# Eight products that nobody reads, put on TensorE at the end of each attention batch

## The chip, the cores and the metric

The kernel runs on one core of one Trainium2 chip. The metric is the device time of that core in microseconds (us), the median over the runs of a kernel. PE is TensorE, DVE is VectorE, ACT is ScalarE, POOL is GpSimd, SP is SyncE.

## The reference

A hybrid block on an array of 16 x 16 x 16 x 64: a gated scan convolution, an attention of 16 heads, and a graph attention that weighs four experts. Only the attention touches the change:

```python
x = x + _L0_conv_ref(_gn(x), ...)
t = _to_tokens(x)                       # 16 batches of 256 tokens, 64 channels
t = t + _L1_attn_ref(_ln_t(t), ...)     # 16 heads of 4 channels
t = t + _L1_ffn_ref(_ln_t(t), ..., edge_index)
...
qkv = (x @ w_qkv + b_qkv).reshape(b, n, 3, H, D)
attn = softmax(einsum('bhqd,bhkd->bhqk', q, k))
out = einsum('bhqk,bhkd->bhqd', attn, v)
```

## The kernel before

Every engine has its own program, written out by hand, and they meet only through semaphores. The attention runs over 16 batches in a software pipeline: in its turn i an engine works on the scores of batch i and on the exponentials and values of batch i - 1. The flags of a turn are `one` (there is a batch i, turns 0 to 15), `two` (there is a batch i - 1, turns 1 to 16) and `three` (there is a batch i + 1).

A turn on PE has eight rounds. A round makes transposed scores of the last batch, two heads each (`scores_t`, L646, into PSUM banks 2 to 5), scores of this batch for two heads (`scores`, L631, banks 0 and 1), in every other round the operands of the next batch (`expand`, L598, bank 7), and the products with the values (`pv`, L615, f32, bank 6). DVE takes the row maxima of each head's scores (L1259) and, beside them, does a piece of a sort that the graph stage needs (`aside`, L1158 and L1159 in the middle batches); POOL prepares that piece. ACT takes the exponentials (L915).

Behind the eighth round the maxima are complete. DVE negates them and splits them into three bf16 parts, a chain of small instructions on which each waits for the last (L1264 to L1285). PE waits for the end of that chain and turns the parts (L669, eight 128-column products):

```python
                if one:

                    pe.wait_ge(mz_ready, i + 1)
                    for g in range(G):
```

DVE adds them to the queries (L1289, `q2`), and `scores_t` of the next turn needs `q2`. PE goes on with the transposes of the last batch's output (L679), then with the first two rounds of the next turn, which have little work since no exponentials are there yet. Behind the attention come the rest of the sort, the experts' products (L730 to L748), and the graph stage. The turns 4 to 12 stand in a hardware loop; between turn 12 and turn 13 all engines do a step of the sort (L687).

Of the kernel before, what the change touches and what calls it, by code (L numbers as in the profile page):

```python
# [23 lines left out]
CH = 512  # L24
# [60 lines left out]
def build(nc, a, cf, cb, jpat, out):  # L85
    ctx = ExitStack()
    with ctx:
# [7 lines left out]
        ps = psum[:]  # L95
# [20 lines left out]
        def select(side, g2):  # L116

            return cB[0:96, (2 * side + g2) * P:(2 * side + g2 + 1) * P]
# [33 lines left out]
        stack = work[0:96, 3:7, :].bitcast(BF16)  # L152
# [184 lines left out]
        def later(i, first):  # L337

            return not isinstance(i, int) or i > first
# [196 lines left out]
        def _(pe):  # L536
# [11 lines left out]
            for w in range(3):  # L548
                if w == 2:
                    pe.wait_ge(s_act, NCH)  # L550
                for c in range(NCH):
                    pe.matmul(ps[:, 4 * (w % 2) + c, :], wbd[:, w, :], xn[:, c * CH:(c + 1) * CH],
                              start=True, stop=True).then_inc(s_z, 1)
# [17 lines left out]
            for c in range(NCH):  # L571
                pe.wait_ge(ln_out, c + 1)
                for u in range(U):
                    pe.matmul(ps[:, u * 4 + c, :], wqkv[C * u:C * u + C, 0:2 * C], tn[C * u:C * u + C, cs(c)],
                              start=True, stop=True).then_inc(s_qk, 1)
            pe.wait_ge(s_qkf, 8)
            for b in range(B):
                for u in range(U):
                    n = b * U + u
# [6 lines left out]
            def expand(i, buf, s):  # L586


                if s > 0:
                    pe.wait_ge(qke_ready, i * 4 + s)  # L590
                elif later(i, 2):
                    pe.wait_ge(o_done, i - 2)
                elif i in (1, 2):
                    pe.wait_ge(qke_ready, 4 * i)
                if s == 0 and isinstance(i, int) and i < 2:
                    pe.wait_ge(stacked[i], STACKED[i])
                for g2 in range(2):
                    mm = pe.matmul(ps[:, 7, g2 * 256:(g2 + 1) * 256], select(s // 2, g2), stack[:, s, bass.ds(i * 256, 256)],  # L598
                                   start=True, stop=True)
                mm.then_inc(ex_ready, 1)  # L600

            def pv(i, buf, m):

                pe.wait_ge(exp_done, i * 8 + m + 1)
                if m == 0:
                    pe.wait_ge(staged, i + 1)
                    if later(i, 0):
                        pe.wait_ge(o_done, i)
                if m == 4:
                    pe.wait_ge(oe_done, i * 2 + 1)  # L610
                g = m // 2
                for kt in range(U):
                    for jj in range(2):
                        j = 2 * (m % 2) + jj
                        mm = pe.matmul(ps[32 * j:32 * j + 32, 6, (g % 2) * 256:(g % 2 + 1) * 256],  # L615
                                       vstage[:, buf, kt, 4 * g + j, :], pbuf[:, m % 4, jj, kt, :],
                                       start=(kt == 0), stop=(kt == 1))
                mm.then_inc(pv_done, 1)

            def scores(i, buf, h):  # L620

                if h == 0:
                    pe.wait_ge(qke_ready, i * 4 + 4)
                if h < 2 and later(i, 0):
                    pe.wait_ge(q2_ready, i * 2 - 1 + h)
                if h >= 2 or later(i, 0):
                    pe.wait_ge(mx_done, i * 16 + h - 1)
                g, j = h // 4, h % 4
                r = slice(32 * j, 32 * j + 32)
                for qt in range(U):  # L630
                    mm = pe.matmul(ps[:, h % 2, qt * 256:(qt + 1) * 256],  # L631
                                   qke[r, buf, 0, g, qt * P:(qt + 1) * P], qke[r, buf, 1, g, :],
                                   start=True, stop=True)
                mm.then_inc(s1_ready, 1)

            def scores_t(i, buf, m):

                if m % 4 == 0:
                    pe.wait_ge(q2_ready, i * 2 + 1 + m // 4)
                if m >= 2 or later(i, 0):  # L640
                    pe.wait_ge(exp_done, i * 8 + m - 1)
                for kt in range(U):
                    for jj in range(2):
                        g, j = m // 2, 2 * (m % 2) + jj
                        r = slice(32 * j, 32 * j + 32)
                        mm = pe.matmul(ps[:, 2 + 2 * (m % 2) + jj, kt * 256:(kt + 1) * 256],  # L646
                                       qke[r, buf, 1, g, kt * P:(kt + 1) * P], q2[r, g, :],
                                       start=True, stop=True)
                mm.then_inc(s2_ready, 1)

            def body(i, buf, one, two, three):
                for m in range(8):
                    if two:
                        scores_t(i - 1, (buf + 2) % 3, m)
                    if one:
                        scores(i, buf, 2 * m)
                        scores(i, buf, 2 * m + 1)
                    if three and m % 2:
                        expand(i + 1, (buf + 1) % 3, m // 2)
                    if two and m >= 1:  # L660
                        pv(i - 1, (buf + 2) % 3, m - 1)
                if two:
                    pv(i - 1, (buf + 2) % 3, 7)
                if one:

                    pe.wait_ge(mz_ready, i + 1)
                    for g in range(G):
                        for qt in range(U):
                            mm = pe.matmul(ps[:, g // 2, (g % 2) * 256 + qt * P:(g % 2) * 256 + (qt + 1) * P],  # L669
                                           mz[:, qt, g, :, :].rearrange("p j r -> p (j r)"), identb, start=True, stop=True)  # L670
                    mm.then_inc(mt_ready, 1)
                if two:

                    pe.wait_ge(oe_done, (i - 1) * 2 + 2)
                    if three:
                        pe.wait_ge(qke_ready, i * 4 + 8)
                    for qt in range(U):
                        for g in range(G):
                            mm = pe.transpose(ps[:, 6 + qt, g * P:(g + 1) * P], ots[:, g, qt * P:(qt + 1) * P], ident)  # L679
                    mm.then_inc(ot_ready, 1)  # L680
# [11 lines left out]
            for g in range(G):  # L692
                expand(0, 0, g)
            pe.wait_ge(s_v1, 2)
            batches(pe, body, turn_slots)
            pe.wait_ge(o_done, B)
            for b in range(B):
# [122 lines left out]
            with pe.If(overflow(pe) > 0):  # L820
                pe.wait_ge(gen_start, 1)
                for u in range(U):
                    for c in range(NCH):
                        mm = pe.matmul(ps[0:NF, 4 * u + c, :], wext[C * u:C * u + C, :], tn[C * u:C * u + C, c * CH:(c + 1) * CH],
                                       start=True, stop=True)
# [15 lines left out]
            for u in range(U):  # L841
                for k in range(8):
                    for q in range(4):
                        r = slice(32 * q, 32 * q + 32)
                        mm = pe.matmul(ps[:, 4 + q, u * 16:(u + 1) * 16], move[r, u, 112 - 16 * k:240 - 16 * k], gv[r, k],
                                       start=(k == 0), stop=(k == 7))
# [797 lines left out]
```

## Time and profile before

| | |
|---|---|
| median of 3 runs | 1025.7 us (1022.24 to 1026.14) |
| the profiled execution | 1031.22 us, its span 1029.5 us |
| PE busy | 644.5 us, 63% of the span |
| DVE busy | 762.1 us, 74% |
| ACT / POOL busy | 306.7 us / 499.9 us |
| mean granted clock of PE | 0.748 |

The page gives busy times of the engines, the clock that PE was granted (1.0 is 2.4 GHz, 0.5 is 1.2 GHz), and the chain of work that ended last. A matmul's time in the profile is that of one product from its start to its end, and products overlap; so a group of eight has a start and a length of its own. "Idle before" names the idle time of the engine just before a group and what ended it.

### The profile page before, as it was taken

The page shows a single profiled execution, that of the slowest core. Times are in us where ns is not written, and L with a number is a line of the kernel's source. Part 1 is how long each engine was busy: PE and PEld are TensorE (multiplying, and loading weights), DVE is VectorE, ACT ScalarE, POOL GpSimd, SP SyncE. Part 2 cuts the span into 40 slices and gives each one's busy share as a digit, 9 for nine tenths or more (in the row PEclk, how much of TensorE's full clock was granted, in tenths as well). Part 3 has the DMA queues.
Part 4 walks back from the last instruction along what each step waited for, and adds up shares of the span by engine and source line. Part 5 has one row for each costly group of instructions (what it writes and reads, how often), then busy time and mean ns, then how long its engine had stood idle before and what let it go on. Part 6 is the DMA issues. An engine that isn't in the chain of part 4 may idle for free.

```text
span 1029.5 us, 15298 instructions
## 1 busy us (share of the span) xinstructions
PE 644.5 (63%) x5984; PEld 331.3 (32%) x5984; DVE 762.1 (74%) x1477; ACT 306.7 (30%) x463; POOL 499.9 (49%) x399
## 2 busy tenths in 40 slices
PE   1501472499788888997787969999999410003421
PEld 1200130133333333333333445555656210002421
DVE  3999887697886877667888779998989831008775
ACT  1510350144554645444444431111111010000015
POOL 3990000017676766650000028888888877756000
PEclk9955875556987977669767969999999855555655
DMA  5010004100000000000000222000000000110001
GB/s 152 0 43 6 8 9 99 24 1 1 1 2 1 1 1 0 0 0 0 2 1 1 82 48 53 6 6 7 6 6 7 7 10 10 10 7 1 3 2 41
DMA packets 22001, 17.08 MB, mean 17 GB/s; under 512 B 13488, under 2 KB 18944, under 8 KB 21168
## 3 DMA queue, kind: packets, MB, share of 16 engines
q1 hardware_dynamic: 15424, 14.02, 5.1%
q0 software_dynamic: 5392, 2.18, 2.6%
q8 instruction: 42, 0.69, 0.3%
q10 hardware_dynamic: 1120, 0.00, 0.1%
q14 instruction: 23, 0.19, 0.1%
HBM read 10.51 MB, written 2.54 MB: 13 GB/s over the span
## 4 chain that ended last, share of the span: by engine, by line
PE 41%; DVE 30%; issue 13%; ACT 4%; SPq 2%; another core or an unknown queue 0%; DMA 0%; DVEq 0%; POOL 0%; ACTq 0%; POOLq 0%
PE psum L615 11%; PE psum L748 10%; DVE mx L1259 7%; PE psum L631 4%; DVE arena L1323 3%; PE psum L646 3%; PE psum L739 3%; PE psum L730 3%; SPq L381 2%; DVE arena L1289 2%; PE psum L598 2%; DVE arena L1030 2%; ACT arena L1004 1%; DVE arena L1026 1%; PE psum L669 1%
## 5 line engine op out<-in xcount | busy, mean ns | idle before, releaser
L493 POOL DMA_INDIRECT work<-node_rows,idx x160 | 257.8, 1611 | 53.1 <-issue 48.5
L1259 DVE TENSOR_REDUCE mx<-psum 128x2 f32<-128x512 f32 x256 | 164.3, 683 | 69.8 <-PE psum L631 67.9
L1323 DVE TENSOR_TENSOR arena<-arena 128x4096 bf16<-128x4096 bf16 (+1 forms) x128 | 182.0, 1486 | 18.1 <-PE psum L748 13.9
L915 ACT ACTIVATE arena<-psum 128x1024 f32<-128x1024 f32 x128 | 129.4, 1024 | 158.4 <-PE psum L646 158.4
L615 PE MATMUL psum<-arena 128*32 128x256 f32 x1024 | 168.3, 486 | 2.3 <-DVE arena L1299 1.4
L470 POOL TENSOR_SCALAR work<-arena,cF 128x184 f32<-128x184 f32 x128 | 93.7, 744 | 129.0 <-DVE arena L1159 73.2
L748 PE MATMUL psum<-arena 128*32 128x128 bf16 x2048 | 131.3, 420 | 4.3 <-DVE arena L1323 3.2
L631 PE MATMUL psum<-arena 32*128 32x256 bf16 x512 | 85.5, 340 | 27.5 <-DVE mx L1259 24.5
L748 PEld LDWEIGHTS psum<-arena 128*32 128x32 bf16 x2048 | 78.2, 149 | 43.6 <-DVE arena L1323 11.6
L615 PEld LDWEIGHTS psum<-arena 128*32 128x32 f32 x1024 | 56.8, 130 | 75.6 <-issue 57.8
L461 POOL COPY arena<-arena 128x160 f32<-128x160 f32 x16 | 5.4, 348 | 136.9 <-DVE arena L1145 91.7
L472 POOL TENSOR_TENSOR work<-work,arena 128x368 f32<-128x368 f32 x64 | 61.8, 965 | 5.3
L790 PE MATMUL psum<-arena,work 128*128 128x32 bf16 x192 | 10.0, 188 | 84.5 <-issue 84.5
L646 PE MATMUL psum<-arena 32*128 32x256 bf16 x512 | 59.9, 331 | 3.0 <-DVE work L1173 1.3
L949 ACT ACTIVATE arena<-psum,b1c 128x512 f32<-128x512 f32 x32 | 21.6, 686 | 133.5 <-PE psum L730 133.5
L1415 DVE COPY work<-psum 92x2048 f32<-92x2048 f32 x1 | 2.3, 2287 | 73.9 <-PE psum L790 73.9
L631 PEld LDWEIGHTS psum<-arena 32*128 32x128 bf16 x512 | 33.4, 113 | 61.6 <-DVE mx L1259 47.1
L412 POOL PARTITION_ALL_REDUCE over<-over x1 | 0.4, 377 | 94.4 <-DVE over L1228 94.4
L598 PE MATMUL psum<-work,arena 96*128 (+1 forms) x128 | 31.3, 336 | 23.8 <-DMA work<-work 21.7
L739 PEld LDWEIGHTS psum<-w,arena 128*128 128x128 f32 x256 | 31.8, 195 | 27.1 <-issue 19.9
L739 PE MATMUL psum<-w,arena 128*128 128x64 f32 x256 | 36.2, 286 | 3.1 <-ACT arena L949 3.1
L560 PE MATMUL psum<-work,cF 128*128 128x512 f32 x8 | 5.2, 804 | 50.5 <-DVE work L1090 50.5
(290 smaller groups left out, 989.7 us busy)
## 6 DMA issues: line engine op xcount, KB each, us to landing
work<-work SPq DMA_DIRECT2D x48, 64.0 KB, 2.0
work<-node_rows,idx POOLq DMA_INDIRECT x160
arena<-in_L_ffn_edge_index_dram SPq DMA_DIRECT2D x2, 1024.0 KB, 10.6
work<-edge_nodes SPq DMA_DIRECT2D x4, 368.0 KB
digits<-arena SPq DMA_DIRECT2D x1, 1024.0 KB, 4.0
arena<-digits SPq DMA_DIRECT2D x1, 1024.0 KB, 4.9
arena<-in_jpat_dram SPq DMA_DIRECT2D x1, 1024.0 KB, 6.8
out_dram<-work SPq DMA_DIRECT2D x4, 256.0 KB, 2.3
```

The lines of the kernel that those rows point to most:

```text
L470: gp.step(pool.tensor_scalar(upto[:, pair % 4, n, :], own, upper[:, 2 * pair + n:2 * pair + n + 1], None, ALU.is_le))
L472: pool.tensor_tensor(upto[:, pair % 4, :, :], upto[:, pair % 4, :, :], own.rearrange("p (n l) -> p n l", n=1).broadcast_to([P, 2, CAP]), A ...
L493: pool.indirect_dma_start(gath[:, l, :], None, tab, bass.IndirectOffsetOnAxis(ap=idx[:, l:l + 1], axis=0)).then_inc(done, 16)
L598: mm = pe.matmul(ps[:, 7, g2 * 256:(g2 + 1) * 256], select(s // 2, g2), stack[:, s, bass.ds(i * 256, 256)], start=True, stop=True)
L615: mm = pe.matmul(ps[32 * j:32 * j + 32, 6, (g % 2) * 256:(g % 2 + 1) * 256], vstage[:, buf, kt, 4 * g + j, :], pbuf[:, m % 4, jj, kt, :], ...
L631: mm = pe.matmul(ps[:, h % 2, qt * 256:(qt + 1) * 256], qke[r, buf, 0, g, qt * P:(qt + 1) * P], qke[r, buf, 1, g, :], start=True, stop=True)
L646: mm = pe.matmul(ps[:, 2 + 2 * (m % 2) + jj, kt * 256:(kt + 1) * 256], qke[r, buf, 1, g, kt * P:(kt + 1) * P], q2[r, g, :], start=True, st ...
L739: mm = pe.matmul(ps[:, 2 + m % 2, t * C:(t + 1) * C], hid[:, m % 4, t * P:(t + 1) * P], w2[:, e, :], start=True, stop=True)
L748: mm = pe.matmul(ps[r, 7, 0:HB], oh[:, buf, HB:HB + LB, c], oh[:, buf, 0:HB, c], start=first and c < 4, stop=last and c >= HC - 4)
L915: act.activation(pbuf[:, m % 4, :, :, :], ps[:, 2 + 2 * (m % 2):4 + 2 * (m % 2), :].rearrange("p j (k q) -> p j k q", k=U), ACT.Exp).then_ ...
L1259: v.reduce_max(mx[:, h, :], ps[:, h % 2, :].rearrange("p (u k) -> p u k", u=U), AX.X).then_inc(mx_done, 1)
L1323: ins = v.tensor_tensor(oh[:, buf, first:first + n, :], hl2[:, s_, bass.ds(blk * HC, HC)].rearrange("p (j c) -> p j c", j=1).broadcast_to( ...
```

## The change

In turns 1 to 15 PE does eight more products between the last `pv` and the wait for `mz_ready`. Each has a stationary operand of 96 x 128 (`select(0, 0)`, bf16) and 512 bf16 columns of `stack`, and writes a PSUM bank from 2 to 5, which holds transposed scores that ACT has read by then. None waits for a semaphore and none raises one. Nothing reads the results: the next `scores_t` writes over them.

```diff
--- before.py
+++ after.py
@@ -661,6 +661,9 @@
                         pv(i - 1, (buf + 2) % 3, m - 1)
                 if two:
                     pv(i - 1, (buf + 2) % 3, 7)
+                if one and two:
+                    for n in range(8):
+                        pe.matmul(ps[:, 2 + n % 4, :], select(0, 0), stack[:, 0, 0:CH], start=True, stop=True)
                 if one:
 
                     pe.wait_ge(mz_ready, i + 1)
```

PE's program around turn 0, `-` before and `+` after; the waits are in brackets, and names behind `<-` are memory (`work` holds `stack`, `arena` the selecting matrices):

```order
 L598 MATMUL psum<-work,arena 128x256 [waits qke_ready]
 L598 MATMUL psum<-work,arena 128x256
-L669 MATMUL psum<-arena,mz 128x128 [waits mz_ready]
-L669 MATMUL psum<-arena,mz 128x128 x7
+L672 MATMUL psum<-arena,mz 128x128 [waits mz_ready]
+L672 MATMUL psum<-arena,mz 128x128 x7
 L646 MATMUL psum<-arena 128x256 [waits q2_ready]
 L646 MATMUL psum<-arena 128x256 x3
```

Turn 0 gets nothing; the lines only have other numbers (L669 is L672 now). The same engine at the end of turn 1:

```order
 L615 MATMUL psum<-arena 32x256 [waits exp_done]
 L615 MATMUL psum<-arena 32x256 x3
-L669 MATMUL psum<-arena,mz 128x128 [waits mz_ready]
-L669 MATMUL psum<-arena,mz 128x128 x7
-L679 MATMUL psum<-cF,arena 128x128 [waits qke_ready,oe_done]
-L679 MATMUL psum<-cF,arena 128x128 x7
+L666 MATMUL psum<-work,arena 128x512 x8
+L672 MATMUL psum<-arena,mz 128x128 [waits mz_ready]
+L672 MATMUL psum<-arena,mz 128x128 x7
+L682 MATMUL psum<-cF,arena 128x128 [waits qke_ready,oe_done]
+L682 MATMUL psum<-cF,arena 128x128 x7
```

The new L666 stands behind the last L615, whose wait for `exp_done` it is queued after, and ahead of the wait for `mz_ready`. This piece is repeated in every turn up to 15. The last turn, 16, gets nothing. The programs of DVE, ACT, POOL and SP are the same but for line numbers.

## Rows read from the trace of the kernel before

**Rows 1.** Page part 2: granted clock of PE in tenths, 40 slices.
```profile
PEclk9955875556987977669767969999999855555655
```

**Rows 2.** Waits of PE: total us, times, longest.
```profile
PE psum L669 <- DVE mr L1285: 30.2, 16, 3.0
```

**Rows 3.** Windows: length, busy us per engine, granted clock, DMA share, GB/s.
```profile
234.00:484.11 250.11, 218.63 (x1673) 91.71 (x1673) 187.90 (x484) 125.97 (x154) 151.54 (x196) 0.77 0.00 1
484.11:577.00 92.89, 74.33 (x566) 32.19 (x568) 79.27 (x254) 40.82 (x47) 0.93 (x2) 0.78 0.00 1
```

**Rows 4.** Windows from one start of L669 to the next.
```profile
345.00:365.06 20.06, 17.10 (x152) 7.54 (x153) 16.91 (x44) 11.38 (x14) 14.75 (x20) 0.91 0.00 0
...
438.04:464.60 26.56, 23.35 (x152) 9.24 (x153) 17.56 (x44) 11.54 (x15) 15.13 (x20) 0.66 0.00 0
464.60:484.11 19.51, 17.12 (x153) 7.62 (x153) 15.58 (x40) 11.38 (x14) 0.35 (x1) 0.91 0.00 0
484.11:512.00 27.89, 20.01 (x164) 8.76 (x165) 24.68 (x80) 11.60 (x14) 0.93 (x2) 0.85 0.00 1
512.00:536.00 24.00, 21.57 (x151) 8.89 (x148) 20.45 (x71) 11.52 (x14) 0.00 (x0) 0.67 0.01 1
536.00:561.50 25.50, 19.29 (x152) 8.91 (x153) 20.69 (x65) 9.17 (x11) 0.00 (x0) 0.80 0.01 1
561.50:577.00 15.50, 13.46 (x106) 5.63 (x105) 13.45 (x39) 8.54 (x9) 0.00 (x0) 0.78 0.01 1
```

**Rows 5.** Windows: the parts of the batch from 345.00 to 365.06.
```profile
345.00:346.60 1.60, 1.54 (x18) 1.31 (x20) 0.89 (x2) 0.00 (x0) 0.62 (x1) 1.00 0.00 0
346.60:350.20 3.60, 2.40 (x24) 0.92 (x26) 3.53 (x11) 2.34 (x3) 0.59 (x1) 1.00 0.00 0
350.20:353.60 3.40, 3.40 (x22) 1.06 (x18) 2.48 (x7) 1.21 (x2) 3.27 (x5) 0.51 0.00 0
353.60:363.36 9.76, 9.76 (x96) 4.24 (x94) 8.50 (x20) 7.24 (x9) 8.64 (x12) 1.00 0.00 0
363.36:365.06 1.70, 0.00 (x1) 0.00 (x1) 1.51 (x9) 0.59 (x1) 1.62 (x3) 1.00 0.00 0
```

**Rows 6.** Timeline, end of that batch: start, us, engine, line, idle before.
```profile
361.90 1.46 PE L615 MATMUL psum<-arena 128*32 128x256 f32 x16
...
364.85 0.15 DVE L1285 COPY mr<-mr 128x1 f32<-128x1 f32 x1
...
365.06 0.62 PE L669 MATMUL psum<-arena,mz 128*128 128x128 bf16 x8 [1.70 <-DVE mr L1285]
```

**Rows 7.** Timeline of DVE: three pairs of maxima in that batch.
```profile
349.42 1.27 DVE L1259 TENSOR_REDUCE mx<-psum 128x2 f32<-128x512 f32 x2
...
352.12 1.29 DVE L1259 TENSOR_REDUCE mx<-psum 128x2 f32<-128x512 f32 x2 [0.92 <-PE psum L631]
...
354.44 1.29 DVE L1259 TENSOR_REDUCE mx<-psum 128x2 f32<-128x512 f32 x2 [0.51 <-PE psum L631]
```

**Rows 8.** Timeline: L669 of two batches that end at half clock.
```profile
233.97 1.03 PE L669 MATMUL psum<-arena,mz 128*128 128x128 bf16 x8 [1.50 <-DVE mr L1285]
...
438.04 1.03 PE L669 MATMUL psum<-arena,mz 128*128 128x128 bf16 x8 [0.61 <-DVE mr L1285]
```

**Rows 9.** Windows around two other falls of the clock.
```profile
389.89:391.20 1.31, 1.31 (x16) 1.26 (x16) 0.58 (x1) 0.00 (x0) 0.00 (x0) 1.00 0.00 0
391.20:404.80 13.60, 12.82 (x74) 4.29 (x74) 8.61 (x22) 6.12 (x7) 7.54 (x10) 0.50 0.00 0
...
438.04:442.40 4.36, 3.23 (x30) 2.14 (x30) 3.15 (x9) 1.91 (x3) 0.00 (x0) 0.89 0.01 2
442.40:459.40 17.00, 16.89 (x92) 5.81 (x94) 9.52 (x22) 7.39 (x10) 11.89 (x16) 0.50 0.00 0
```

**Rows 10.** The chain of work: L703, eight passes of 512 f32 columns.
```profile
582.21 3.44 PE psum L703 x8
```

**Rows 11.** Page part 5: the maxima on DVE, busy us, mean ns, idle before.
```profile
L1259 DVE TENSOR_REDUCE mx<-psum 128x2 f32<-128x512 f32 x256 | 164.3, 683 | 69.8 <-PE psum L631 67.9
```

## The prediction

> **What bounds the kernel now.** I read the page first, then the waits of PE, then windows cut at the starts of L669, then the timeline of one batch. The page's clock line shows the attention (slices 9 to 22, 26 us each) at 5 to 9 tenths: PE changes between its two levels, 2.4 GHz (1.0) and 1.2 GHz (0.5), all the time [rows 1]. The windows say how much: over the eleven batches from 234.00 to 484.11 the granted clock is 0.77, over the rest of the attention 0.78 [rows 3]. A mean of 0.77 means that (1 - 0.77) x 2 = 46% of 250.11 us, 115 us, ran at half clock.
>
> What half clock costs is seen by comparing batches. The one from 345.00 to 365.06 takes 20.06 us at 0.91; the one from 438.04 to 464.60 takes 26.56 us at 0.66. DVE works 16.91 and 17.56 us in them, nearly the same [rows 4]. So the difference is PE: at half clock a round is bound by PE, and DVE waits for scores; at full clock DVE is nearly the bound.
>
> The batch from 345.00 shows where the clock is lost [rows 5]. L669 and L679 fill PE up to 346.60. Then it is thinly used (2.40 of 3.60 us), because the first rounds wait for DVE's `q2` and maxima and have no values to multiply. At 350.20 the clock falls, for 3.40 us. Then 9.76 us of unbroken work at full clock, and at the end PE sits idle for 1.70 us, waiting for the negated maxima; this wait occurs 16 times, 30.2 us in all, 3.0 us at most [rows 2]. So in each batch there are two thin places, the idle one ahead of L669 and the one behind L679, with only 1.6 us of dense work between. What PE did before a fall: in this batch the second thin place, after the first. At 391.20 the clock fell only 1.3 us behind L669, right behind the idle place [rows 9]. The batch from 345.00 also had such a wait ahead of it (16 waits in 16 turns [rows 2]), and yet stayed at 1.00 until 350.20 [rows 5]: there the idle place alone did not drop the clock. I conclude that both thin places count together, and the change fills the first one.
>
> **The new products' own cost.** Each has 512 columns, eight have 4096. L669 has 8 x 128 = 1024 columns and takes 0.62 us at full clock [rows 6], 1.03 at half [rows 8]; the 0.41 between is what 1024 columns gain by twice the clock, so they cost 0.43 at 2.4 GHz and 0.85 at 1.2. Four times that: 1.71 us at full clock, 3.41 at half. An upper bound at full clock: the eight f32 passes of 512 columns at L703 take 3.44 us [rows 10]. I take 1.71, since these are bf16 as L669 is. Their weight loads lie beside the products as L669's do.
>
> At full clock the last value product ends at 363.36, and L669 starts at 365.06, 0.06 after the 0.15 us of L1285 from 364.85 have ended [rows 6]. The idle time is 1.70, the new work 1.71. It just fits; queued behind it are L669 and, through `q2`, all of the next batch. I take 0.1 us of delay a batch, bounds 0 and 0.3: 14 x 0.1 = 1.4 us. At half clock 3.41 us meet idle times of 1.50 and 0.61 [rows 8]: 1.9 to 2.8 us late. Turn 1 arrives at half clock (L669 takes 1.03 at 233.97). The dense work may raise the clock on its way, as it did inside the L669 and L679 of 438.04 (0.89 over 4.36 us [rows 9]); I take 1.0, bounds 0 and 1.9.
>
> **What a batch costs when the clock stays up.** In the batch from 345.00, three pairs of maxima start at 349.42, 352.12 and 354.44, with waits of 0.92 and 0.51 for PE [rows 7]. Taking those waits away gives 1.4 us: 20.06 - 1.4 = 18.66. DVE's 16.91 us fit into that, with 1.75 left for its own waits. For the batch from 464.60, 19.51 - 1.4 = 18.1. So eleven batches take 10 x 18.66 + 18.1 = 204.7 instead of 250.1: **45.4 us** saved. Divided by 115 us at half clock, that is 0.40 us for each us.
>
> The Trainium skill ("TensorE: Matmul & The Clock Gate", Terms) prices throttled time at that time x (1 - K/N), one half. By it the saving would be 57 us. The rows say less, (26.56 - 20.06) us for some 14.5 us more of half clock, 0.45, and DVE's busy time forbids the rest.
>
> The four last windows of the attention are closer to DVE's limit, because `aside` is a longer sort there: DVE works 24.68 of 27.89, 20.45 of 24.00, 20.69 of 25.50, 13.45 of 15.50 us [rows 4]. Leaving DVE its 1.75 us of waits in each, they can give 1.5, 1.8, 3.1 and at most 0.3; with 0.3 to 1 for the last, since its fall at the start comes from the same idle place, I take **7 us** together. If these wait on DVE for other reasons, it is 2.
>
> The other engines lose nothing: ACT works 11.38 us of a batch and POOL 14.75 [rows 4], both below 18.66; but POOL comes to 79% there, and if its pieces came late DVE would wait for it. The banks that are written over are read by then. What follows the attention moves forward as a whole; its own clock I leave as it is, give or take 3 us.
>
> **The sum.** 45.4 + 7 - 1.4 - 1.0 = 50.0. The profiled execution took 1031.22 us: 981.2. Its median neighbours took 1025.7, 5.5 us less; if their half-clock time was the same, they would land at 975.7, and if those 5.5 us were more half-clock time, which would vanish as well, at 981.2. I take the middle, **979**.
>
> **The rivals.** A difference under 0.5% (5.1 us) can't be told from no change here.
>
> A, the forecast: the clock stays up from turn 1 or 2 until the attention ends. 62%. Own range 968 to 992.
>
> B, the thin place behind L679 is enough by itself, as long as it follows any other work. For it: in the batch of 438.04, which came at half clock with only 0.61 us idle ahead of L669, the clock rose and fell again at 442.40 [rows 8, 9]. Against it: that batch had come from half clock, not from full. Then each batch keeps one stretch of 3.40 us and comes back quickly because it never goes deeper: 10 x 20.06 + 19.51 = 220.1, 30.0 saved, 4 in the late turns, less 2.4: 32 saved, 994 to 999. 22%.
>
> One rule speaks for B: the Trainium skill (same page, PE-mode transpose) says that transposes don't count as PE being busy. L679 is such transposes, and by that rule the thin place would begin 0.6 us behind L669's start and not 1.6, longer than the new work can make up for. No row here separates L679 from L669.
>
> C, nothing changes in the pattern of the clock: falls and long stretches at half clock as in 391.20 to 404.80 and 442.40 to 459.40 [rows 9] come as before. Then only the delays are left, 15 x 0.1 to 0.3, 1027 to 1030. 8%.
>
> D, slower: batches arrive at half clock more often than now, so that the new products take 3.41 us. It pays 1.9 to 2.8 us in each such turn, against nothing gained; it decides when more than about three batches of 15 arrive so while the others gain nothing. If all do: 15 x 2.4 = 36, about 1060; with half of them about 1043. Against it: of the rows, 345.00 and 464.60 ended at full clock, and dense work ahead of the wait makes half clock less likely. 8%.
>
> **How the numbers follow.** A, B, C, D: 62, 22, 8, 8. Faster by over 0.5% is A and B, 84%, less a little for a B that gives back its gain: 0.83. Within 0.5% is C and that little: 0.09. Slower: 0.08. The range from 968 to 1004 holds A and B nearly whole, 80%.
>
> **What would show it.** In the profile after: the clock line at 9 from slice 9 to 21, and 1.00 in windows of a batch (B: 0.91 in all; C: 0.77). Starts of L672 18.7 us apart. The idle time ahead of L672 near 0 instead of 1.70. L666 in 120 products, groups of eight 1.7 to 1.9 us long. L1259's idle time before it down from 69.8 us [rows 11] to some 30. DVE near 90% busy in the attention. I am wrong if PE still shows half clock behind the thin place (B), if L672 starts over 0.5 us after L1285 has ended (the new work doesn't fit), or if POOL's pieces become what DVE waits for.

## The result and the profile after

The changed kernel takes 1031.95 us (median of 5 runs, 1030.9 to 1034.82) where the kernel before takes 1025.7 (median of 5 runs, 1022.24 to 1033.62). The ratio is 1.010, with a 95% interval from 1.006 to 1.014: 1% slower. The profiled execution took 1034.82 us, its span 1033.1. Every ratio below is to executions of the kernel before that were taken beside that run, and their medians were 1028.6 to 1031.8 us, so ratios can be compared and times only roughly. The ratios leave out executions in which the chip was in a slower state, while the medians hold them: two of the four with 14 products (1075.1 and 1086.3 us), one of the four with short products (1038.1) and two of the kernel before.

A turn is measured here from one start of L672 to the next (L669 before), and has the number of the turn whose body it holds: turn 2 runs from the L672 of turn 1 to that of turn 2. The late turns are 13 to 16.

The page after, busy time and granted clock of PE in 40 slices; the clock line answers to [rows 1]:

```profile
PE 667.7 (65%) x6104; PEld 337.7 (33%) x6104; DVE 761.7 (74%) x1477; ACT 306.7 (30%) x463; POOL 498.7 (48%) x399
...
PEclk8755785556669968689899969999999855556655
```

There is no run of nines from slice 9 on, as I had forecast. PE is busy for 23 us more, with the new work, and its clock goes up and down as before. The windows that answer to [rows 3], turns 2 to 12 and the late turns:

```profile
235.03:490.67 255.64, 241.10 (x1762) 100.02 (x1760) 186.99 (x484) 126.03 (x154) 150.59 (x196) 0.77 0.00 1
490.67:580.00 89.33, 73.40 (x591) 31.02 (x591) 79.31 (x254) 40.86 (x47) 0.93 (x2) 0.90 0.00 1
```

The granted clock of turns 2 to 12 is 0.77, the same as before, and they take 255.64 us in place of 250.11. The parts of one turn that answer to [rows 5]:

```profile
334.14:335.74 1.60, 1.54 (x19) 1.31 (x20) 0.87 (x2) 0.00 (x0) 0.64 (x1) 1.00 0.00 0
335.74:339.60 3.86, 2.66 (x26) 1.01 (x26) 3.79 (x11) 2.52 (x3) 0.84 (x2) 0.99 0.00 0
339.60:343.00 3.40, 3.40 (x22) 1.12 (x20) 2.57 (x7) 1.02 (x1) 3.23 (x5) 0.50 0.02 5
343.00:352.27 9.27, 9.27 (x94) 4.13 (x90) 8.01 (x17) 7.24 (x9) 8.22 (x11) 1.00 0.00 0
352.27:354.15 1.88, 1.88 (x10) 0.70 (x9) 1.65 (x10) 0.58 (x1) 1.80 (x4) 1.00 0.00 0
```

The last part is the wait for the maxima: PE is busy 1.88 of 1.88 us where it was idle for 1.70. The second part is the thin place behind L682 (L679 before), 2.66 of 3.86 us; behind it the clock falls, 5.4 us behind the start of L672, where it was 5.2. Filling the wait changed nothing about the fall. Windows cut at each change of the clock show such a fall in each of the turns 2 to 12, between 5.0 and 5.9 us behind L672. The kernel before had one fall in each of these turns too: ten lie 4.4 to 7.0 us behind L669, and only that of 391.20 [rows 9] is close behind the idle wait.

The turns that answer to [rows 4]:

```profile
235.03:262.00 26.97, 25.77 (x161) 10.21 (x160) 17.36 (x48) 11.56 (x14) 17.18 (x23) 0.62 0.00 1
...
289.35:314.06 24.71, 23.29 (x161) 9.27 (x159) 17.59 (x44) 11.50 (x14) 14.76 (x19) 0.72 0.01 2
314.06:334.14 20.08, 18.82 (x160) 8.35 (x161) 16.91 (x44) 11.37 (x14) 14.10 (x19) 0.92 0.01 1
```

Five turns take 20.0 to 20.1 us, with 3.4 us at half clock. Three take 24.7 with 13.6, and three 26.97, 27.35 and 26.98 with 20.5. Before, five had 3.4 us as well, and six had long stays: four of 13.6, one of 17.1 and one of 20.5. The five take 100.2 us in both kernels, the six 150.0 before and 155.4 after: the whole difference lies in them. The one with 20.5 us before:

```profile
412.90:438.04 25.14, 23.27 (x153) 9.18 (x153) 16.86 (x44) 11.55 (x14) 15.43 (x20) 0.61 0.00 0
```

It took 25.14 us, where the change takes 26.97 to 27.35 with the same stay. That is the new price. The timeline of PE, in a turn that arrives at full clock and in one that arrives at half:

```profile
332.38 1.90 PE L666 MATMUL psum<-work,arena 96*128 96x512 bf16 x8
334.14 0.62 PE L672 MATMUL psum<-arena,mz 128*128 128x128 bf16 x8
```

```profile
286.92 2.59 PE L666 MATMUL psum<-work,arena 96*128 96x512 bf16 x8
289.35 0.61 PE L672 MATMUL psum<-arena,mz 128*128 128x128 bf16 x8
```

At full clock L672 starts at 334.14, before the group of L666 has quite ended (334.28), since products overlap: the new work fits into the wait. Where the turn arrives at half clock, L666 takes 2.59 us, though the clock rises inside it, and L672 waits for it. DVE waits for PE at L1292; the same line before and after:

```profile
DVE arena L1289 <- PE psum L669: 14.7, 16, 1.2
```

```profile
DVE mx L1262 <- PE psum L631: 67.0, 57, 11.8
DVE arena L1292 <- PE psum L672: 19.8, 16, 2.9
```

So 5.1 us went to that, all of it in turns 2 to 12. The waits for scores (L1262 <- L631) are 67.0 us and were 67.9. The sum of the difference in span, 3.6 us: 0.5 up to the end of turn 0 (L672 at 203.50, L669 at 203.01), where nothing new has run yet, 0.6 in turn 1, 5.5 in turns 2 to 12, 3.5 gained in turns 13 to 15, and 0.6 lost behind them. The clock of the late turns is 0.90 and was 0.78 [rows 3].

### The profile page after: what moved, and what is told of

Read it like the earlier page. It is cut to its first block, busy times and chain, and to the rows that moved or that the text cites. A ratio compares the mean times of both kernels' runs of the same rounds, so it can differ in the third digit from the quotient of the medians.

```text
span 1033.1 us, 15538 instructions
## 1 busy us (share of the span) xinstructions
PE 667.7 (65%) x6104; PEld 337.7 (33%) x6104; DVE 761.7 (74%) x1477; ACT 306.7 (30%) x463; POOL 498.7 (48%) x399
## 4 chain that ended last, share of the span: by engine, by line
PE 46%; DVE 26%; issue 10%; ACT 4%; another core or an unknown queue 3%; SPq 2%; DMA 0%; DVEq 0%; POOL 0%; ACTq 0%; POOLq 0%
PE psum L615 13%; PE psum L751 11%; DVE mx L1262 5%; PE psum L631 3%; PE psum L646 3%; PE psum L733 3%; PE psum L742 3%; DVE arena L1326 3%; SPq L381 2%; DVE arena L1292 2%; PE psum L598 2%; PE psum L666 2%; DVE arena L1033 2%; ACT arena L1007 1%
## 5 line engine op out<-in xcount | busy, mean ns | idle before, releaser
L1262 DVE TENSOR_REDUCE mx<-psum 128x2 f32<-128x512 f32 x256 | 164.4, 684 | 68.6 <-PE psum L631 67.0
L1326 DVE TENSOR_TENSOR arena<-arena 128x4096 bf16<-128x4096 bf16 (+1 forms) x128 | 182.1, 1487 | 17.1 <-PE psum L751 16.9
L615 PE MATMUL psum<-arena 128*32 128x256 f32 x1024 | 168.0, 490 | 2.8 <-DVE arena L1302 2.2
L631 PE MATMUL psum<-arena 32*128 32x256 bf16 x512 | 85.7, 335 | 30.5 <-DVE mx L1262 27.3
L615 PEld LDWEIGHTS psum<-arena 128*32 128x32 f32 x1024 | 57.3, 130 | 74.1 <-issue 55.2
L646 PE MATMUL psum<-arena 32*128 32x256 bf16 x512 | 60.1, 322 | 3.0 <-DVE work L1176 1.3
L631 PEld LDWEIGHTS psum<-arena 32*128 32x128 bf16 x512 | 33.3, 111 | 65.3 <-DVE mx L1262 50.3
```

The lines of the kernel that those rows point to most:

```text
L631: mm = pe.matmul(ps[:, h % 2, qt * 256:(qt + 1) * 256], qke[r, buf, 0, g, qt * P:(qt + 1) * P], qke[r, buf, 1, g, :], start=True, stop=True)
L1262: v.reduce_max(mx[:, h, :], ps[:, h % 2, :].rearrange("p (u k) -> p u k", u=U), AX.X).then_inc(mx_done, 1)
L1326: ins = v.tensor_tensor(oh[:, buf, first:first + n, :], hl2[:, s_, bass.ds(blk * HC, HC)].rearrange("p (j c) -> p j c", j=1).broadcast_to( ...
```

## The experiments

The theories, named as the expectations name them. T1: the thin place behind the transposes drops the clock by itself. T2, the theory of the prediction: both thin places count together, so enough dense work ahead holds the clock. T3: the transposes don't count as work. T4 and T5 came from the runs: the clock changes only at certain moments, which do not follow the turn; whether a turn falls, and for how long, depends on where these moments lie in it. T4 expects a fall wherever they let the thin place count; T5 says of the run with 16 products that its turn length keeps them off the thin place.

**Four products in the thin place, none at the end.**

```diff
                     if two:
                         scores_t(i - 1, (buf + 2) % 3, m)
+                    if one and m == 1 and later(i, 1):
+                        pe.wait_ge(o_done, i - 1)
+                        for n in range(4):
+                            pe.matmul(ps[:, 6 + n % 2, :], select(0, 0), stack[:, 0, 0:CH], start=True, stop=True)
```

> The kernel before, and four unread 512-column products in turns 2 to 15, not at the end of the turn but in the thin place behind L679: ahead of the third head's scores, behind a wait for the last output. T1 (the thin place behind L679 drops the clock by itself): the fall at 5 us behind L669 goes in most turns, and what is left are falls about 1 us behind it from the idle wait; 985 to 1010 us. T2 (both thin places count together): the wait at the end is as idle as before, falls stay at about 1 or 5 us behind L669, 1020 to 1030. If neither place matters, 1026 to 1030, half clock for as long as before.

Measured: 999.2 us, ratio 0.974 (0.968 to 0.980). Windows of a turn without a fall, and of the next with its parts:

```profile
277.11:296.34 19.23, 16.57 (x156) 7.63 (x157) 17.30 (x44) 11.38 (x14) 14.75 (x20) 1.00 0.01 1
296.34:297.00 0.66, 0.66 (x10) 0.66 (x11) 0.00 (x0) 0.00 (x0) 0.64 (x1) 0.98 0.00 0
297.00:300.30 3.30, 3.28 (x22) 1.88 (x21) 2.86 (x8) 1.09 (x2) 0.00 (x0) 0.50 0.02 5
296.34:316.06 19.72, 17.52 (x157) 8.29 (x157) 17.54 (x44) 11.38 (x14) 14.75 (x20) 0.91 0.01 2
```

Of the turns 3 to 12, four stay at full clock throughout, 19.2 to 19.6 us each. There are five falls. One lies 4.8 us behind the turning of the maxima (L669 before). The other four lie at the idle wait, one in it and three up to 0.9 us behind it, as here, 0.66 us. So the idle wait can drop the clock too, without a thin place behind it. T1 had both: the falls at 5 us go in most turns, those from the idle wait are left, and the time lies in its range. T2 had 1020 to 1030 us. So filling the second place alone already takes most falls away.

**Both places filled** (the change, and these four).

> The change, and the four products of the thin place as well. T1: no fall in turns 2 to 12, a turn takes 18.7 us, 975 to 990 us in all. T2: the same, since both places are filled. T3 (the transposes L679 do not count, so that the thin place starts earlier and is too long for four products): falls stay in a part of the turns, 1000 to 1030. Against all three: if the clock still falls 5 us behind L669 in every turn, four products are too little or the place of the fall has another cause.

Measured: 990.8 us, ratio 0.965 (0.961 to 0.970). The thin place of one turn, then turns 2 to 12:

```profile
314.93:318.53 3.60, 3.21 (x28) 1.23 (x30) 3.53 (x11) 2.33 (x3) 0.58 (x1) 1.00 0.00 0
235.22:447.38 212.16, 203.78 (x1805) 92.30 (x1804) 188.59 (x484) 125.15 (x154) 150.13 (x195) 0.99 0.00 1
```

The thin place is busy 3.21 of 3.60 us. Eleven turns take 212.16 us at 0.99, most of them 19.23; one of the eleven fell. That is 38 us less than the 250.11 of before in these turns, most of the 45.4 that I had forecast for the change alone. The time is just above the 975 to 990 us that T1 and T2 had, since a turn takes 19.2 us and not 18.7.

**The same instructions with almost no work**: the four products of the thin place have 32 columns.

```diff
-                            pe.matmul(ps[:, 6 + n % 2, :], select(0, 0), stack[:, 0, 0:CH], start=True, stop=True)
+                            pe.matmul(ps[:, 6 + n % 2, 0:32], select(0, 0), stack[:, 0, 0:32], start=True, stop=True)
```

> The kernel of the change with four products in the thin place, but these four have 32 columns in place of 512: the same instructions, wait and order, almost no work. If it is the work in the thin place that holds the clock, the falls at 5 us come back and the kernel takes 1020 to 1035 us. If it was the order or the wait for the last output that helped, it stays at 986 to 995.

Measured: 1030.8 us, ratio 0.999 (0.990 to 1.008); the profiled execution 1020.3. One turn, turns 2 to 12, and the place of the fall in turn 5:

```profile
313.24:340.22 26.98, 25.98 (x166) 10.31 (x165) 16.86 (x44) 11.57 (x14) 15.42 (x20) 0.62 0.01 1
234.29:476.75 242.46, 230.39 (x1805) 98.37 (x1804) 187.35 (x484) 125.82 (x154) 150.47 (x195) 0.82 0.00 1
298.29:301.70 3.41, 3.41 (x22) 1.18 (x18) 2.38 (x6) 1.28 (x2) 3.33 (x5) 0.50 0.00 0
```

The same place of turn 5 with the 512 columns (both places filled):

```profile
299.28:302.69 3.41, 3.41 (x36) 1.46 (x34) 3.29 (x8) 2.18 (x4) 3.31 (x5) 1.00 0.00 0
```

The falls at 4.7 to 5.9 us are back in nine of the eleven turns. It is the work in the thin place that holds the clock, not the wait or the order. Nor is it a lucky turn length: the two kernels go alike through turns 2 to 4 (19.22, 19.59 and 20.05 us here, 19.21, 19.59 and 20.08 with 512 columns), and both fall in turn 4, 4.7 and 4.8 us behind the turning of the maxima (L672 in the change). In turn 5 this one falls again, 5.1 us behind it; the other, at 5.2 us, does not.

**Sixteen at the end**, `range(16)` in place of `range(8)`.

> The change with 16 products in place of 8 at the end of the turn. T1: falls stay at 5 to 6 us behind L669 and the turn is longer by the 1.5 to 1.7 us that no longer fit into the wait (3.4 at half clock): 1055 to 1075 us. T2: the dense work ahead holds the clock up in a part of the turns, a turn takes 18.7 + 1.6 = 20.3 us: 1000 to 1025.

Measured: 1004.5 us, ratio 0.980 (0.975 to 0.986). One turn, and turns 2 to 12:

```profile
297.58:317.99 20.41, 19.16 (x169) 8.91 (x168) 17.26 (x44) 11.37 (x14) 14.71 (x19) 1.00 0.00 1
235.86:460.91 225.05, 210.96 (x1849) 98.10 (x1848) 188.65 (x484) 125.04 (x154) 148.71 (x193) 1.00 0.00 1
```

No fall in eleven turns. By my expectations this was T2. But nine turns in a row take 20.42 us, and the three counts around it say otherwise.

**Twelve, fourteen and eighteen at the end.**

> The change with 12 products at the end. A turn without half clock takes 19.5 us, so the moments at which the clock can change move through the turn, and cannot stay beside the thin place, as they may have in the run with 16. T4: falls at 5 to 6 us behind L672 in a third to a half of turns 2 to 12, none in the others; 1000 to 1020 us. T2: no falls in these turns, since the dense work ahead holds the clock up wherever they lie; 985 to 995 us.

Measured: 1044.3 us, ratio 1.014 (1.008 to 1.021). Two turns and turns 2 to 12:

```profile
328.66:349.52 20.86, 19.60 (x165) 8.80 (x164) 16.85 (x44) 11.38 (x14) 14.77 (x19) 0.92 0.01 2
349.52:373.24 23.72, 22.48 (x166) 9.36 (x165) 16.95 (x44) 11.43 (x14) 14.76 (x19) 0.78 0.00 0
235.87:486.23 250.36, 236.29 (x1806) 101.00 (x1805) 185.70 (x484) 125.55 (x154) 149.48 (x194) 0.83 0.00 1
```

Every turn of 2 to 12 falls, 4.1 to 5.2 us behind L672. T2 is refuted here, since this is 50% more dense work than the change has; T4's "a third to a half" was too few.

> The change with 14 products at the end. With 16 no turn of 2 to 12 fell, with 12 each did. Either 16 is dense enough (T2), or the turn of 20.42 us happened to keep the thin place off the moments at which the clock can change (T5). A turn without a fall would take about 20.0 us here, which does not hold still. T5: falls 4 to 6 us behind L672 in most turns, 1025 to 1045 us. T2: no or few falls, 990 to 1005 us.

Measured: 1069.9 us, ratio 1.030 (1.020 to 1.040). A turn and turns 2 to 12:

```profile
354.60:381.83 27.23, 26.09 (x168) 10.27 (x167) 17.49 (x44) 11.51 (x14) 14.80 (x19) 0.69 0.00 0
235.07:504.54 269.47, 255.69 (x1827) 106.73 (x1826) 187.38 (x484) 125.87 (x154) 149.50 (x194) 0.78 0.00 1
```

Nine of the eleven turns fall, 3.9 to 4.7 us behind L672, which is what T5 has and T2 has not. The time is longer than T5's 1045 us even in the fastest execution (1055.0), since the stays at half clock are long, up to 23.9 us.

> The change with 18 products at the end: denser ahead of the thin place than with 16, and a turn without a fall of 20.85 us, which does not hold still as 20.42 did. T2: no falls in turns 2 to 12, 1008 to 1016 us. T5: falls return in most or all of the turns, 22 to 24 us a turn, 1025 to 1055 us.

Measured: 1039.2 us, ratio 1.010 (1.003 to 1.017). A turn without a fall, the half-clock part of the next, that turn, and turns 2 to 12:

```profile
305.89:326.74 20.85, 19.60 (x172) 9.12 (x170) 17.26 (x44) 11.37 (x14) 14.71 (x19) 1.00 0.00 1
...
332.70:346.30 13.60, 13.60 (x80) 4.65 (x76) 7.65 (x17) 6.80 (x8) 10.63 (x15) 0.50 0.00 0
326.74:353.30 26.56, 25.30 (x172) 10.30 (x171) 17.50 (x44) 11.51 (x14) 14.74 (x19) 0.74 0.01 1
237.19:489.81 252.62, 238.55 (x1871) 105.09 (x1870) 189.56 (x484) 125.63 (x154) 148.23 (x193) 0.89 0.00 1
```

With 18 the pattern is regular from turn 4 on: two turns of 20.85 us without a fall, then one that falls 6.0 us behind L672 and takes 26.56. I expected falls in most turns and got four in eleven; but they come, with more dense work ahead than in the run with 16. So 16 isn't enough work, it is a turn length that stays clear (T5).

**Ten at the end.**

> The change with 10 products at the end in place of 8. T4 (the fall comes in every turn whose thin place the chip looks at whole, and how soon the clock comes back depends on where in the turn the fall lies): the falls stay, but a turn is about 0.35 us longer than 20.05, so that the fall stays near 5.0 to 5.4 us behind L672, from where the clock came back after 3.4 us in the change; most turns of 2 to 12 take 20.4 us, 1000 to 1012 us in all, although there is more unread work. T2 (both thin places count together): at best a part of the falls goes, 18.7 + 0.4 us in such turns, 985 to 1010 with turns free of half clock. If only the work counts: 1032 to 1037.

Measured: 1018.5 us, ratio 0.988 (0.981 to 0.994). Up to the fall and behind it in one turn, then turns 3 to 12:

```profile
303.54:308.60 5.06, 3.81 (x39) 2.20 (x39) 4.27 (x12) 2.19 (x3) 0.69 (x2) 1.00 0.00 0
308.60:312.00 3.40, 3.40 (x24) 1.17 (x18) 2.34 (x6) 1.36 (x2) 3.32 (x5) 0.51 0.00 0
...
262.23:467.28 205.05, 192.16 (x1621) 85.94 (x1620) 167.81 (x436) 113.76 (x140) 133.55 (x173) 0.92 0.00 1
```

Nine turns in a row take 20.47 us, and each falls 5.1 to 5.2 us behind L672 and comes back 3.4 us later. T4 had this, in 1000 to 1012 us; turn 2 (27.4 us) and the late turns kept long stays. Two unread products more than in the change make a kernel that is faster than the change, and with 0.988 faster than the kernel before, though every turn still falls. The same turn length without any fall was the run with 16. So the amount of work at the end is not what decides.

**The transposes as products.**

```diff
-                            mm = pe.transpose(ps[:, 6 + qt, g * P:(g + 1) * P], ots[:, g, qt * P:(qt + 1) * P], ident)
+                            mm = pe.matmul(ps[:, 6 + qt, g * P:(g + 1) * P], ots[:, g, qt * P:(qt + 1) * P], ident, start=True, stop=True)
```

> The change, with the eight transposes L679 of a turn done as f32 products with the identity, which gives the same numbers. T3 (transposes do not count): the dense stretch behind the wait becomes 1.6 us longer for PE's activity, the falls 5 us behind L669 go in most turns: 985 to 1010 us. T1: the falls stay, and the longer products (about 1.7 in place of 1.04 us) cost 0 to 0.7 us a turn: 1032 to 1043 us.

Measured: 1015.5 us, ratio 0.989 (0.984 to 0.993). One turn, turns 2 to 12, and the half-clock stays of three turns in a row:

```profile
298.21:318.85 20.64, 19.39 (x169) 9.35 (x168) 17.00 (x44) 11.38 (x14) 14.65 (x20) 0.92 0.00 1
233.38:468.95 235.57, 221.85 (x1849) 104.51 (x1848) 186.10 (x484) 125.30 (x154) 150.94 (x196) 0.88 0.00 1
303.70:307.11 3.41, 3.41 (x22) 1.31 (x20) 2.17 (x6) 1.50 (x2) 3.33 (x5) 0.50 0.00 0
324.18:327.59 3.41, 3.41 (x21) 1.30 (x22) 2.01 (x5) 1.48 (x2) 3.33 (x5) 0.50 0.02 5
344.66:348.07 3.41, 3.41 (x20) 1.17 (x20) 1.95 (x5) 1.24 (x2) 3.30 (x5) 0.50 0.00 0
```

All eleven turns fall, 4.9 to 5.5 us behind L672: T3 is refuted as the reason for the falls. The time went down all the same, against both theories' numbers, because eight of the eleven stay at half clock for only 3.4 us and such a turn takes 20.6 to 20.8. It is the run with ten over again. The falls also show that the moments do not follow the turn: here they come 20.48 us apart while these turns take 20.65 us, so that they creep forward in the turn, from 5.5 to 5.3 and 5.2 us behind L672; in the run with ten they come 20.48 us apart as well, with turns of 20.47 us.

**Dense work in the fourth round**, eight products ahead of `expand`'s own, beside the change.

```diff
+                if s == 1 and later(i, 1):
+                    for n in range(8):
+                        pe.matmul(ps[:, 7, :], select(0, 0), stack[:, 0, 0:CH], start=True, stop=True)
                 for g2 in range(2):
```

> The change, and eight products more in each turn's fourth round, some 8 us behind L672, where PE is at half clock after the fall. Dense work there should bring the clock back. T4: falls stay in the turns as in the change, but each is followed by a rise within 3.4 to 6.8 us; a turn takes 20.1 plus 1.7 to 3.4 us for the products, 21.8 to 23, in place of 22.6 on the average: 1015 to 1040 us. If the long stretches at half clock had another cause than how dense PE's rounds are, they stay, and the kernel takes 1050 to 1060.

Measured: 1010.2 us, ratio 0.984 (0.976 to 0.991), below both ranges. Turns 2 to 12, and a late turn:

```profile
233.86:459.29 225.43, 211.33 (x1849) 97.27 (x1849) 184.31 (x484) 126.37 (x154) 151.79 (x196) 1.00 0.00 1
487.94:516.77 28.83, 25.53 (x168) 10.03 (x168) 21.89 (x80) 11.60 (x14) 0.00 (x0) 0.76 0.01 1
```

This did not test what it was made for: there was no fall in turns 2 to 12, whose length of about 20.46 us again stays clear, as in the run with 16. Whether a dense burst ends a stay at half clock is open; in turn 14 the eight products did not shorten one of 13.7 us.

**Six in the thin place, from turn 1 on**, beside the change.

> The change, and six products in the thin place behind L682 in turns 1 to 15 (four in turns 2 to 15 gave 990.8 us). If four were just short of enough: the last fall of turns 2 to 12 goes, and those of turns 13 to 15 too; half clock saved there is worth up to 5 us, six products cost 0.3 us more a turn (the heads' scores wait for them), 4 us: 984 to 994 us. If turns 13 to 15 fall for their own waits on DVE, 992 to 998.

Measured: 995.0 us, ratio 0.966 (0.961 to 0.972). Turns 2 to 12, then turn 13 with the step of the sort ahead of it:

```profile
234.39:446.01 211.62, 204.95 (x1827) 93.11 (x1826) 188.15 (x484) 125.16 (x154) 150.75 (x196) 1.00 0.00 1
446.01:477.63 31.62, 28.05 (x176) 11.15 (x174) 24.89 (x80) 11.52 (x14) 0.93 (x2) 0.68 0.00 1
```

No fall in turns 2 to 12, and 211.62 us, 0.5 less than with four. What was gained is lost in turn 13: 31.62 us, 2.5 more than with four. The late turns, not the middle ones, are what is left in the attention. Of the 3.6 us by which this profiled execution is longer than that with four, 3.1 lie behind the attention, where the programs are the same (clock 0.75 there, and 0.76).

**The step of the sort filled as well.** With four products in the thin place, PE waits twice between turns 12 and 13, ahead of L694 (the sort's transposes) and ahead of turn 13's L646:

```profile
450.57 1.06 PE L694 MATMUL psum<-cF,arena 128*128 128x128 f32 x8 [1.70 <-DVE over L1174]
452.96 0.64 PE L646 MATMUL psum<-arena 32*128 32x256 bf16 x6 [1.32 <-DVE work L1180]
```

```diff
             def turn_slots():
 
+                for n in range(8):
+                    pe.matmul(ps[:, 2 + n % 4, :], select(0, 0), stack[:, 0, 0:CH], start=True, stop=True)
                 pe.wait_ge(q2_ready, 2 * (B - 3))
...
                 mm.then_inc(slots_turned, 1)
+                for n in range(5):
+                    pe.matmul(ps[:, 2 + n % 4, :], select(0, 0), stack[:, 0, 0:CH], start=True, stop=True)
```

> The change with four full products in the thin place (990.8 us), and 13 unread products more in the step of the sort between turns 12 and 13, where PE is idle 1.70 and 1.32 us (eight ahead of that step's transposes, five behind them). There the clock fell and stayed at half for 13.7 us. If the idle places feed that fall: it goes, and 3 to 6 us are saved, 984 to 988. If turn 13's waits on the sort in DVE make it: 989 to 994.

Measured: 988.5 us, ratio 0.961 (0.955 to 0.967). Turns 2 to 12 and turn 13:

```profile
233.76:445.06 211.30, 202.56 (x1805) 92.04 (x1804) 188.96 (x484) 125.15 (x154) 150.70 (x196) 1.00 0.00 1
445.06:471.90 26.84, 23.85 (x186) 10.24 (x185) 24.68 (x80) 11.71 (x14) 0.93 (x2) 1.00 0.00 1
```

Turn 13 takes 26.84 us at full clock, and took 29.12; the time is just above the 984 to 988 us expected if the fall goes. The intervals of this run and of the 990.8 overlap, so the kernels can't be told apart by time; the turn can. This is the best version measured: 4% faster than before, with more than 180 unread products.

## Why the prediction was wrong

**What bounds the kernel: right.** PE's half clock is what DVE waits for. Turns at full clock take 19.2 us with the thin place filled, where my sum had 18.66, and eleven of them save 38 us against the forecast 45.4. So the saving would have been about 6 us too large even with the clock up. The four products' work is not the reason, since turn 2 of the control with 32 columns takes 19.22 us as well; the sum took two waits off one turn and had no row of a turn at full clock.

**The step that failed** is the sentence "I conclude that both thin places count together, and the change fills the first one". It rested on one kind of row: idle waits behind which the clock had stayed up. The changed kernel has the first place filled, 1.88 of 1.88 us, and falls in each of the turns 2 to 12. Runs with twelve products fall in each of them too. Filling the second place alone leaves five falls in ten turns, four of them at the idle wait, and filling both leaves one in eleven, and the control with 32 columns brings nine back. The row that spoke against the step stood in my own rows: the turn of 438.04, with only 0.61 us idle ahead of L669, rose and fell again behind the thin place [rows 8, 9]. I had set it aside because that turn had come from half clock.

**Rival C was the outcome, for B's reason.** C, at 8%, had falls and long stays come as before, a clock of 0.77 and 1027 to 1030 us; measured are 0.77 and 1031.95. It gave no reason why. B, at 22%, had it: the thin place is enough by itself. It had the fall stay in every turn, as it did, but took one stretch of 3.40 us as the price of a fall, from one turn [rows 5]. In the trace after, five falls of eleven cost 3.4 us, three 13.6 and three 20.5; its sign, a clock of 0.91, did not come. The rows had shown stays of 13.6 and 17.0 us too [rows 9]. Nothing in the change shortens them.

**D's price was right, and it is what made the kernel slower.** Three of the turns 2 to 12 arrive at the new work at half clock, and DVE waits up to 2.9 us for L672 there, where the mean of before was 14.7 / 16 = 0.9; 5.1 us more in all, nearly the 5.5 by which these turns grew. Such a turn takes 26.97 to 27.35 us where the one with the same stay took 25.14, 1.8 to 2.2 more; I had 1.9 to 2.8. I held it for unlikely (8%) that this would meet turns that gain nothing.

**The new work's own cost: right.** L666 takes 1.90 us as a group at full clock, in which the last product's end overlaps L672; I had 1.71 for its columns, and L672 is not late. Turn 1, which arrives at half clock: 31.53 us where it took 30.96, 0.6 more, 1.0 forecast.

**The late turns: right in direction.** Their clock went from 0.78 to 0.90, and 3.5 us came back; I had 7. Here the change did what I had thought of it. Before, three falls lay at the idle wait, one in it and two up to 0.8 us behind it, the first with 17.1 us at half clock; after, no fall of the attention is closer behind L672 than 4.1 us. The first of the three, while PE waits for the maxima ahead of the L669 of 511.64:

```profile
510.66:511.64 0.98, 0.00 (x1) 0.01 (x1) 0.82 (x6) 0.00 (x0) 0.00 (x0) 0.50 0.00 0
```

So the idle wait does drop the clock in some turns, and filling it takes these falls away; in turns 2 to 12 there was only one of them.

**The rule on transposes** (the Trainium skill, "TensorE: Matmul & The Clock Gate", PE-mode transpose) is not what made the falls: with the transposes done as ordinary products they stay where they were. The price of half clock by the Trainium skill ("TensorE: Matmul & The Clock Gate", Terms), one half, was too high: turns 2 to 12 with 0.77 and with 0.99 to 1.00 differ by 38 us at 115 us of half clock, 0.33.

**What stays open.** Why a stay at half clock lasts 3.4 us in one turn and 20.5 in the next isn't shown. PE counts as busy all through it in either case. That it goes with where in the turn the fall lies is seen. In turns 2 to 12 of the traces before, after and of the 32-column control every fall from 4.7 to 5.4 us behind L672 has 3.4 us at half clock, and every fall from 5.5 on has 13.6 or 20.5. With ten products nine falls in a row at 5.1 us have 3.4. But falls at 5.5 have 3.4 where the transposes are products, and falls at 3.9 to 4.7 with 12 or 14 products have 3.4 to 24. The runs give no rule that would have told the times of the runs with 12, 14 or 18.

## What to carry to other kernels

Where the granted clock of a kernel goes up and down, look at what PE does in the few microseconds ahead of each fall, and fill that place, which need not be the one that is most idle; a control with the same instructions and few columns tells whether it is the work that counts. A kernel that repeats one period can fall into step with the moments at which the clock changes: then a few tenths of a microsecond more or less in the period move the time by several per cent in either direction, so try several amounts before a result is put down to the edit. Unread work that fits at full clock doesn't fit at half, so its cost must be counted at the clock at which the turn arrives.

## What was not expected of the hardware

The time does not follow the amount of work. With 8, 10, 12, 14, 16 and 18 products at the end of each turn the ratios to the kernel before are 1.010, 0.988, 1.014, 1.030, 0.980 and 1.010; those with 8, 12 and 18 can't be told apart. Two kernels whose turns take 20.42 and 20.47 us hold still, one at full clock throughout (16), one with a fall 5.1 us behind L672 in every turn (10).
